# Combining a mixture-of-experts output with attention rows in expert order: a recurrent block on one core

## What is computed

```python
s = attention(xn)          # 4 heads of 32; decay matrix from gates; each head's row
                           # normalised to mean 0, variance 1, times gamma = 1 + ln_w
top1 = argmax(xn @ router_w + router_b)        # one of E = 8 experts per token
h = xn @ w1[e] + b1[e]; a, g = split(h)        # 128 -> 2 x 512
y = (a * sigmoid(g)) @ w2[e] + b2[e]           # 512 -> 128
out = x + s * silu(y)
```

## Time and profile before

| | us |
|---|---|
| median of 3 runs | 240.97 |
| lowest, highest | 240.56, 242.08 |
| the profiled execution | 240.99 |
| its span, first to last instruction | 239.2 |

### The profile page before, as it was taken

How to read it: one execution, slowest core, us unless ns; L and a number is a source line. 1 busy time by engine, 2 the same in 40 slices (tenths; PEclk the granted TensorE clock), 3 DMA queues, 4 the chain that set the end, 5 groups by cost and what they waited for, 6 DMA issues and landing times.

```text
span 239.2 us, 6066 instructions
## 1 busy us (share of the span) xinstructions
PE 209.1 (87%) x1824; PEld 170.8 (71%) x1832; DVE 181.8 (76%) x505; ACT 136.5 (57%) x313; POOL 100.0 (42%) x128
## 2 busy tenths in 40 slices
PE   0688879689999999979999999999999999999650
PEld 0568744335555555559999999999999999986310
DVE  6997378299989986648777988898889789671490
ACT  0276756779788796754555555555555655540110
POOL 7553200027777776000333364425533464366150
PEclk9988999999999999999999999999999999999975
DMA  6999999501441111401097021102101000000994
GB/s 175 266 419 418 282 299 394 221 3 46 146 137 53 49 53 59 115 21 33 15 261 204 26 58 52 55 22 62 44 30 50 28 25 25 26 11 13 251 315 137
DMA packets 29730, 29.30 MB, mean 122 GB/s; under 512 B 3295, under 2 KB 24807, under 8 KB 29697
## 3 DMA queue, kind: packets, MB, share of 16 engines
q1 hardware_dynamic: 26258, 24.59, 33.0%
q0 software_dynamic: 2272, 4.22, 5.4%
q10 hardware_dynamic: 1168, 0.10, 0.4%
HBM read 20.01 MB, written 9.34 MB: 123 GB/s over the span
## 4 chain that ended last, share of the span: by engine, by line
PE 67%; DVE 11%; issue 6%; ACT 5%; DMA 5%; DVEq 1%; SPq 1%; POOL 1%; ACTq 0%; POOLq 0%
PE bank L1195 13%; PE head_bank L1195 13%; PE bank L1204 12%; PE head_bank L1159 5%; PE bank L1169 5%; PE bank L1149 4%; PE head_bank L1052 4%; PE bank L1180 3%; PE bank L1148 3%; DMA xw<-y_tokens 2%; DVE stats L696 2%; PE bank L1037 2%; PE bank L1082 2%; DVE cm L859 2%; PE head_bank L1131 1%
## 5 line engine op out<-in xcount | busy, mean ns | idle before, releaser
L449 POOL DMA_INDIRECT y_tokens<-ffn,idx x39 | 39.2, 1004 | 76.3 <-DVE ffn L992 74.0
L443 POOL DMA_INDIRECT xs_sorted<-xw,pos x32 | 33.0, 1031 | 36.3 <-DVE pos L831 26.9
L1204 PE MATMUL bank<-w_sb,dm 128*128 x312 | 41.3, 275 | 0.5 <-DVE dm L976 0.5
L1195 PE MATMUL bank<-xsT,wc 128*128 128x128 f32 x320 | 39.3, 276 | 0.1
L1204 PEld LDWEIGHTS bank<-w_sb,dm 128*128 128x128 f32 x312 | 38.0, 192 | 0.7 <-issue 0.7
L1195 PEld LDWEIGHTS bank<-xsT,wc 128*128 128x128 f32 x320 | 37.4, 192 | 0.5 <-DVE wc L851 0.3
L1195 PE MATMUL head_bank<-xsT,wc 128*128 128x128 f32 x304 | 37.0, 275 | 0.0
L1195 PEld LDWEIGHTS head_bank<-xsT,wc 128*128 128x128 f32 x304 | 35.4, 192 | 0.0
L859 DVE TENSOR_TENSOR cm<-dm,head_bank 128x1024 f32<-128x1024 f32 (+1 forms) x32 | 29.0, 948 | 6.3 <-ACT dm L586 3.5
L600 ACT ACTIVATE wc<-w_sb 128x512 f32 x39 | 24.6, 630 | 14.3 <-issue 14.3
L586 ACT ACTIVATE dm<-bank 128x512 f32<-128x512 f32 x48 | 26.9, 594 | 4.5 <-PE bank L1149 3.5
(11 more groups left out here) (199 smaller groups left out, 352.0 us busy)
## 6 DMA issues: line engine op xcount, KB each, us to landing
x_sb<-in_L_attn_x SPq DMA_DIRECT2D x16, 256.0 KB, 5.1
w_sb<-in_L_ffn_w SPq DMA_DIRECT2D x8, 512.0 KB, 8.2
wc<-in_L_ffn_w SPq DMA_DIRECT2D x5, 512.0 KB, 17.1
xs_sb<-xs_sorted SPq DMA_DIRECT2D x13, 193.5 KB, 2.8
xs_sorted<-b_sb SPq DMA_DIRECT2D x1, 2048.0 KB, 17.3
xw<-y_tokens SPq DMA_DIRECT2D x8, 256.0 KB, 4.6
out_x<-xw SPq DMA_DIRECT2D x8, 256.0 KB, 3.6
y_tokens<-ffn,idx POOLq DMA_INDIRECT x39, 2.3
```

What stands on the lines that cost most here:

```text
L443: pool.indirect_dma_start(xs_dram, bass.IndirectOffsetOnAxis(ap=pos[:, t:t + 1], axis=0), xw[:, t, :], None).then_inc(s_scat, 16)
L449: pool.indirect_dma_start(y_dram, bass.IndirectOffsetOnAxis(ap=idx[:, j:j + 1], axis=0), ys_sb[:, j // CH % 2, j % CH, :], None, bounds_ch ...
L1195: last = pe.matmul(bank[2 * (j % 2) + k][:, c * P:(c + 1) * P], wc[:, j % 3, m:m + P], xsT[:, j % 2, :], start=True, stop=True)
L1204: last = pe.matmul(bank[6 + j % 2][:, 0:D], uT[:, j % 2, c, :], w2_sb[:, bass.ds(e * (HC * D) + c * D, D)], start=(c == 0), stop=(c == HC ...
```

## The change

The output is put together in expert order. The tensor `y_tokens`, its load, the products and sums in token order and the stores go. In their place:

- a DRAM tensor `s_sorted` (4992 rows of 256 floats: s beside x), which SP fills with zeros behind `b1`'s load
- `x_sb`, `xnT` and the new s share one buffer `qk`; x is loaded again into its odd halves behind the fourth piece of `xs_sorted`
- the squares are made by ACT (8 of 128x512, in iterations 0 to 3); `normalise` has two groups of 16 tiles in quarters, 31 steps each: 4 sums, 19 small ones (128x64), and for each quarter the product with the coefficients and the product with gamma. DVE takes four steps per iteration
- POOL scatters each tile's [s, x] row by `pos` into `s_sorted` (32 scatters of 128 rows of 1 KB) as quarters are ready; SP loads that back in 13 pieces
- `combine(c, ...)` on DVE, two operations over 3 blocks (128x384): times s, plus x. It is placed in iterations `COMBINE_AT` = 24, 25, ..., 33, 35, 38, and for the last piece block by block in 38, 39, 40. POOL scatters the sum straight into the output, one scatter of 128 rows per block, in order behind its s scatters
- gate: `Tanh` with scale 0.5, and the product adds 1 (`scalar_tensor_tensor`), `add_bias` halves; SiLU is one ACT instruction with `Silu` instead of a Sigmoid and a product on DVE
- DVE and ACT wait for the xs scatters before the expert stage, since `yall` (ten slots of three blocks) lies over `xw`.

```diff
-    GROUPS = [(0, 4), (4, 4), (8, 4), (12, 4)]
-    NSTEPS = 25
-    GAMMA_AT = (9, 18, 27, 34)
+    GROUPS = [(0, 8), (8, 8)]
+    NQ = 4
+    SMALL_STEPS = NQ + 19
+    NSTEPS = SMALL_STEPS + 2 * NQ
+    NSLOT = 10
+    NSS = 4
+    COMBINE_AT = [max(24 + c, CH * c + 5) for c in range(NCH - 1)]
...
             sp.dma_start(w1_sb[P - 1:P, :, :], b1.unsqueeze(0)).then_inc(s_b1, 16)
+            sp.wait_ge(s_zero, 1)
+            sp.dma_start(ss_dram.rearrange("(p n) d -> p n d", p=P),
+                         zeros[:, :].unsqueeze(1).to_broadcast([P, NBLK, S])).then_inc(s_ssf, 16)
...
+            def load_s(c):
+                if c >= NSS:
+                    sp.wait_ge(s_cb, c - NSS + 1)
+                sp.dma_start(ss[:, c % NSS, :, :, :].rearrange("p n k d -> p n (k d)"),
+                             ss_dram[c * CH * P:(c + 1) * CH * P, :].rearrange("(n p) d -> p n d", p=P)).then_inc(s_ssl[c], 16)
...
-                if c == NX + 1:
+                if c == NX - 1:
                     sp.wait_ge(s_sc, B)
-                    for g in range(NPC):
-                        ts = slice(g * TP, (g + 1) * TP)
-                        sp.dma_start(x_sb[:, ts, :], x_t[:, ts, :]).then_inc(s_xr, 16)
...
+                    for g in range(XG):
+                        ts = slice(g * TG, (g + 1) * TG)
+                        sp.dma_start(sx[:, ts, 1, :], x_t[:, ts, :]).then_inc(s_xr, 16)
+                if c == NCH - 3:
+                    sp.wait_ge(s_ss, 16 * T)
+                    sp.wait_ge(s_ut, B)
+                    for i in range(NSS):
+                        load_s(i)
+                if c == NCH - 2:
+                    load_s(NSS)
+                    load_s(NSS + 1)
+            for i in range(NSS + 2, NCH):
+                load_s(i)
...
+            pool.wait_ge(s_ssf, 16)
+            pool.wait_ge(s_xr, 16 * XG)
+            for t in range(T):
+                g, i = t // GT, t % GT
+                pool.wait_ge(s_norm, NSTEPS * g + SMALL_STEPS + 2 * (i // QT + 1))
+                pool.indirect_dma_start(ss_dram, bass.IndirectOffsetOnAxis(ap=pos[:, t:t + 1], axis=0),
+                                        sx[:, t, :, :].rearrange("p n d -> p (n d)"), None).then_inc(s_ss, 16)
+
+            for c in range(NCH):
+                for n in range(CH):
+                    j = CH * c + n
+                    if c < NCH - 1:
+                        pool.wait_ge(s_cb, c + 1)
+                    else:
+                        pool.wait_ge(s_cb, NCH + n)
+                    pool.wait_ge(s_idx, c + 1)
+                    pool.indirect_dma_start(out_rows, bass.IndirectOffsetOnAxis(ap=idx[:, j:j + 1], axis=0),
+                                            yall[:, c % NSLOT, n, :], None, bounds_check=NTOK - 1, oob_is_err=False).then_inc(s_ost[min(c, NCH - NSLOT)], 16)
...
-                               ACT.Sigmoid).then_inc(s_th, 1)
+                               ACT.Tanh, scale=0.5).then_inc(s_th, 1)
...
-                    act.preload_act_table_set("sigmoid_and_others")
+                    act.preload_act_table_set("silu_and_others")
...
+            def squares(i):
+                ts = slice(i * QT, (i + 1) * QT)
+                act.wait_ge(s_sc, B)
+                act.wait_ge(s_oe, (i + 1) * QT // 2)
+                act.activation(sall[:, ts, :, :], u_all[:, ts, :, 0:DH], ACT.Square).then_inc(s_sq, 1)
...
+                act.activation(yall[:, c % NSLOT, n, :], yb[:, j % 2, :], ACT.Silu).then_inc(s_ye, 1)
...
-                dve.tensor_tensor(uT[:, j % 2, :, :].rearrange(flat), bank[2 * (j % 2)][:, :], sg[:, j % 2, :, :].rearrange(flat),
-                                  ALU.mult).then_inc(s_uu, 1)
+                dve.scalar_tensor_tensor(uT[:, j % 2, :, :].rearrange(flat), sg[:, j % 2, :, :].rearrange(flat), 1.0,
+                                         bank[2 * (j % 2)][:, :], ALU.add, ALU.mult).then_inc(s_uu, 1)
...
+            def combine(c, n0, n1):
+                y = yall[:, c % NSLOT, n0:n1, :]
+                dve.wait_ge(s_ye, CH * c + n1)
+                dve.wait_ge(s_ssl[c], 16)
+                dve.tensor_tensor(y, y, ss[:, c % NSS, n0:n1, 0, :], ALU.mult).then_inc(s_mix, 1)
+                mixed[0] += 1
+                dve.wait_ge(s_mix, mixed[0])
+                dve.tensor_tensor(y, y, ss[:, c % NSS, n0:n1, 1, :], ALU.add).then_inc(s_cb, 1)
...
-                if j >= 2:
-                    silu(j - 2)
-
-                step(normals)
-            while step(normals):
-                pass
-
-            finish()
+                if j in COMBINE_AT:
+                    c = COMBINE_AT.index(j)
+                    combine(c, 0, CH)
+                if j >= NBLK - 1:
+                    combine(NCH - 1, j - NBLK + 1, j - NBLK + 2)
+
+                step(normals, 2)
```

More of the change, by code:

```diff
@@ L169, in mlstm_moe_block @@
         pick = dflat[:, 1536:2304].bitcast(BF16).rearrange("p (j n m) -> p j n m", j=NBS, n=3)
-        sqs = [cflat[:, i * GT * D:(i + 1) * GT * D].rearrange("p (t h d) -> p t h d", t=GT, h=NH) for i in range(2)]
         ssum = sb("ssum", [P, GT * NH])
@@ L236, in mlstm_moe_block @@
         s_ye = sem("s_ye")
-        s_yst = [sem(f"s_yst{i}") for i in range(NX)]
-        s_yg = [sem(f"s_yg{i}") for i in range(NPC)]
+        s_ssl = [sem(f"s_ssl{c}") for c in range(NCH)]
+        s_ost = [sem(f"s_ost{i}") for i in range(NCH - NSLOT + 1)]
+        s_ss = sem("s_ss")
+        s_ssf = sem("s_ssf")
+        s_xr = sem("s_xr")
+        s_cb = sem("s_cb")
+        s_sq = sem("s_sq")
+        s_mix = sem("s_mix")
         s_norm = sem("s_norm")
@@ L643, in _, with silu @@
                     copy_w(1)
+            def silu(j):
+                c, n = j // CH, j % CH
+                act.wait_ge(s_yb, j + 1)
+                if c >= NSLOT and n == 0:
+                    act.wait_ge(s_ost[c - NSLOT], 16 * CH)
+                act.activation(yall[:, c % NSLOT, n, :], yb[:, j % 2, :], ACT.Silu).then_inc(s_ye, 1)
[4 more added lines that the diff above has]
+                act.activation(sall[:, ts, :, :], u_all[:, ts, :, 0:DH], ACT.Square).then_inc(s_sq, 1)
+            act.wait_ge(s_scat, 16 * T)
             for j in range(NBLK + 2):
@@ L647, in _ @@
                     evac_xs(j + 1)
+                if j < NQ:
+                    squares(2 * j)
+                    squares(2 * j + 1)
                 if 1 <= j < NBLK - 1:
@@ L652, in _ @@
                 if j >= 2:
-                    act.wait_ge(s_yb, j - 1)
-                    if j >= 4:
-                        act.wait_ge(s_ye, j - 3)
-                    act.activation(sy[:, j % 2, :], yb[:, j % 2, :], ACT.Sigmoid).then_inc(s_sy, 1)
-            for i, g in enumerate(PE_PIECES):
-                act.wait_ge(s_sum, i + 1)
-                act.activation(yg[:, g * TP:(g + 1) * TP, :], bank[i][:, :].rearrange("p (t d) -> p t d", d=D), ACT.Copy).then_inc(s_fina, 1)
+                    silu(j - 2)
         @block.vector
@@ L1000, in _ @@
             dve.wait_ge(s_w2, 32)
+            dve.wait_ge(s_scat, 16 * T)
             normals = normalise_all(range(len(GROUPS)))
```

125 lines of the change are left out of this document (31 added, 94 removed).

## The result

The kernel after takes 244.56 us (median of 4, 243.82 to 245.35) beside 241.50 for the kernel before (median of 4, 240.56 to 242.08): ratio 1.0151, interval 1.0111 to 1.0190. The forecast was 232.5 with a range to 238.5; the change makes the kernel slower by 3.1 us, a small loss but clear of the interval. The profiled execution took 245.35 us with a span of 243.5, against a forecast span end of 230.7.

A forecast was written before the change was run, and what follows sets the result against it. PE bounds the kernel before; afterwards POOL's queue of 39 output scatters: first at 178.0, plus 38 x 1.30 to 227.4, landed 229.5, span 230.7, time 232.5. Forecast's own range 229 to 237 (chance 0.63); with rival 1 and another, 226.5 to 238.5.

The forecast's parts named there:

- The tail: End of the kernel: the old 18.2 us tail goes; after the last scatter lands at 229.5, the span ends at 230.7.
- DVE in the expert stage: Expert-stage iterations of 2.5 us with four small steps, 3.6 with four heavy ones; PE loses 0.3 us net, bounds 0 to 4.
- three times 0.86 late: Heavy steps in iterations 6 to 8: DVE falls behind PE by 0.86 us three times and 0.2 more, 2.8 us.
- The slot of 1.30: POOL's output scatters back to back: each takes 0.98 us busy plus 0.30 idle, taken as 1.30 us per slot.
- rival 1: POOL's output slots are stretched beside two-source DVE work to a mean of 1.44: +5.3 us, 237.8; chance 0.15.
- Behind combine(0): Iteration 24: hidden(24) at 172.75, combine(0) done at 177.2, first output scatter at 178.0.
- The s scatters: POOL's 32 scatters of s: last starts near 168.4, loaded back by 173.8, covered with 2.3 us before combine(0); cost 0.
- Rival 3: Scatters of s with 1 KB rows are dear, 2.26 us a slot: combine(0) +26.7 us, time 259; chance 0.06.
- scalar_tensor_tensor: DVE's product and bias by this instruction: no difference taken; upper bound 0.53 us more for a second pass over 512 elements.
- rival 4: DVE becomes the bound with 0.53 us more per product, some +9 us on combine(0): 241.5; chance 0.04.
- Edits costed at nothing: Tanh and Silu, ACT's squares, the fill (13 to 18 us, covered) and the x reload: cost 0 each.
- rival 5: Tanh and Silu lie in different table sets, two loads of 1.28 us per block: about +100 us, 330; chance 0.02.

The follow-up runs named there:

- e_before_nopool: The kernel before with the three sums that POOL makes in its tail given to DVE: 239.48 us, 0.9916 of the kernel before.
- e_before_drain: The kernel before with one DRAIN added on POOL behind its 32 xs scatters, where POOL is idle: 239.22 us, 0.9919 of the kernel before.
- e_drain: The kernel after with one DRAIN added on POOL behind the 32nd s scatter, where POOL is idle: 239.25 us, 0.9935 of the kernel before.
- e_no_gamma: The kernel after without the eight gamma products on DVE (s isn't multiplied by gamma): 242.17 us, 1.0047 of the kernel before.
- v1_groups_b: The kernel after with DRAINs behind xs and s scatters, groups of 20 and 12 tiles, combines two iterations earlier; repeat run: 234.86 us, 0.9738 of the kernel before.
- e_before_silu_b: The kernel before with only the Tanh gate, scalar_tensor_tensor product and bias, and one-instruction Silu; repeat run: 241.01 us, 0.9988 of the kernel before.

## Why the prediction was wrong, by its steps

The forecast of a span of 230.7 missed by 12.8 us: 6.4 at the end, 4.5 at the first output scatter, 1.8 in the slots.

*The tail: "so the span ends 1.24 us after a last landing".* This is the step that failed. The end of the span was priced from SP's last wait alone, and the interval from the last store's landing to the end was carried over as if it belonged to the landing. In fact 1.0 us of it was SP waiting, at the end of the program, for POOL's DRAIN; the wait is gone in e_before_nopool and e_before_drain. When POOL gets 32 scatters more and becomes the last to work, this wait grows to 7.3. The end cost 243.5 - 233.75 = 9.75 us against 3.3 forecast. e_drain shows the cause: one DRAIN in an idle stretch takes 5.3 us off it, and with 39 scatters behind it the end is 4.5.

*DVE in the expert stage: "0.3 net", bounds 0 to 4.* PE lost 4.2 us, just above the upper bound; DVE was the bound from iteration 8 to 18. That this costs something was seen, and its size was wrong by two durations: small iterations 2.7 to 3.0 us behind the first heavy run instead of 2.5, heavy ones 3.93 instead of 3.6. The sum took the old iterations' durations and added and subtracted whole operations, the added heavy step at 0.65. Left out was that the added step is chained to its neighbour: heavy pairs go at 0.71 and 0.75 instead of 0.60, and in small iterations the pair pushes the read of the expert out from under `silu`'s product. (The sum's "three times 0.86 late" isn't its own 3.6 less 2.79 either, which is 0.81; that changes the term by 0.2 us.) Of the 4.2, e_no_gamma gives back 2.7; that DVE bound is shown by it, the part of the chained pair is read from rows only. Another 0.6 us of the late start (108.83 against 108.24) belong to neither: by PE's timeline, hidden(1) lay between 107.2 and 109.2 in kernels whose work up to there is that of before or after.

*The slot of 1.30.* 1.348; +1.8 us. Right was that POOL's queue binds, at 0.98 + 0.30, and that rival 1 (two-source work on DVE) is there; it is a third as large as that rival's price of 5.3.

*Behind combine(0).* From hidden(24) to the first output scatter 4.95 us were forecast, and it took 5.02. The step from DVE's end to the scatter, the two operations of 0.55 and the wait between them were right.

*The s scatters.* Rival 3 fell on its price: busy time with 1 KB rows is that of 512 B rows. The first came at 127.87 (forecast 127.1), the second group's at 152.70 (148.9 worked out, after 3.95 us of waiting for a late DVE), the last at 172.42. SP's load was issued at 175.07, and combine(0), itself late, never met it. That is no test of the margin of 2.3 us, since DVE made both late; in v1_groups_b, where combine(0) comes two iterations earlier, it waited 2.0 us.

*scalar_tensor_tensor.* The product took 680 ns, the old one 681: rival 4's mechanism is false. Its result, that DVE sets PE's pace for a stretch and the gain is gone, came nearer the truth than the forecast, by another way. The rule quoted from the Trainium skill, "Vector Engine (DVE) Microarchitecture Reference", section "Points that are easy to get wrong", speaks of two SBUF sources. The product has one of its two in PSUM, so its 680 ns neither bear the rule out nor speak against it; only the 291 and 291 ns of the earlier trace rows disagree with it.

*Edits costed at nothing.* Tanh and Silu cost nothing (e_before_silu_b, and no load of tables between the blocks: rival 5 is false); the squares stopped nothing either, as blocks 1 to 7 keep their 2.79 us; the fill took 20.6 us instead of 13 to 18 and was still covered; the reload of x too.

*What stays open.* What a DRAIN works off for 0.083 us per scatter isn't shown; the lengths follow the number of scatters whatever their rows' bytes. Nor is it shown what costs PE the 1.4 us that it still loses without the gamma products. Left untried: v1 with DVE's small steps spread thinner, so that combine(0) need not wait for s.

## What to carry to other kernels

Where a change moves the last work to another engine, read how the span ends for every engine: the last rows at the end of the program, who drains how long, and whom the others wait for. A wait that is put down to an engine that was done long ago is a sign that another one isn't finished. On POOL, count the indirect DMAs since its last DRAIN and place a DRAIN where it is idle; none belongs into a full queue. And when steps are packed denser on an in-order engine, take the length of a dense iteration with its gaps from a row as dense, or give the term a bound above its sum; ask above all what a chained pair holds up behind it, such as a register load.

## What the runs showed of the hardware that was not expected

- POOL's closing DRAIN ends 0.083 us per indirect scatter (128 rows each) behind its last operation: 3.2 us for 39, 8.5 for 103, in the kernel after 7.2 us after the data has landed. A DRAIN sets the count back: in e_drain the closing one is as long as 39 scatters make it, not 103. With 3 scatters it takes 1.3, and in a full queue each leaves at least 2.2 us idle. Amid the kernel one behind 32 scatters took 2.8 to 4.4.
- Most indirect scatters of 128 rows take 0.96 to 0.98 us with rows of 512 B, 516 B and 1 KB alike, and the next begins 0.30 later; in the kernel after, six that start within 0.2 us behind the start of a combine on DVE take 1.23 to 1.36.
- Before a copy whose source is chosen by a register, DVE's sequencer reads the register from memory in 0.30 us, and where nothing else holds it the copy starts 0.7 to 0.8 us after that read began; what DVE still has queued covers it, and an operation that waits for the one just before it doesn't let the read begin (0.51 us idle before the copy instead of 0.30 to 0.36).
